# Squares turned by VectorE instead of TensorE transposes, and x loaded without its zeros, in a graph kernel on one core

## The chip, the cores and the metric

The kernel runs on one core of one Trainium2 chip. The metric is the device time in microseconds (us) of one execution. The core's engines are TensorE (PE; PEld is its loading of weights), VectorE (DVE), ScalarE (ACT), GpSimd (POOL) and SyncE (SP), which here issues most of the DMAs.

## What is computed

For each of B = 2048 samples, x is a 50 by 32 matrix (N nodes, D features). T = 2 maskers make an adjacency each, whose rows are divided by their sum; one step of a gated recurrence runs over the graph; batch and layer normalisation and an attention pooling follow. Cut to what matters:

```python
adj = einsum('bn,tnm->btm', x.reshape(b, 1600), masker_param) + masker_bias
adj = relu(adj).reshape(b, t, n, n)
adj = adj / (adj.sum(axis=-1, keepdims=True) + 1e-06)
m = einsum('btnd,de->btne', h, weight)
m = einsum('btnm,btmd->btnd', adj, m)
gates = m @ w_ih.T + b_ih + h @ w_hh.T + b_hh
# r, z, ng: sigmoid, sigmoid, tanh(r * ng)
h = (1.0 - z) * ng + z * h
# then normalisation over the batch, over the sample, softmax pooling over n
```

## The kernel before, in words

The samples are 16 tiles of 128. The program has three stages, each a block in which the engines run their own instruction streams against semaphores; between the blocks all engines meet.

**Stage 1** (`stage1`) computes the adjacency. The 100 rows of the two maskers are cut in 10 groups of GN = 10 rows, 500 columns wide; the tiles are cut in 2 blocks of 8. A *window* is one tile with one group: 160 windows, numbered c. In a window TensorE issues 38 matmuls of 128x500 (`window`, L445; x and the weights are each split in a high and a low part, `x_hi`, `x_lo`, `w_hi`, `w_lo`). ScalarE applies relu from PSUM into `u` (L307), VectorE sums the rows, adds epsilon, takes the reciprocal and multiplies into `an` (`normalise`, L357 to L365). `an` has the samples on its partitions. The next stage needs the column node m there, so TensorE turns it: after the fourth of its seven units of matmuls, window c runs four transposes of window c-1 (`transposes`, L427; 125 columns each), ScalarE copies them from PSUM to `at` (`evacuate`, L313), and SP stores `at` to the DRAM tensor `adjT` (`store_tile`, L204). The last window's transposes follow the loop. `u`, `an`, `at` and their PSUM banks are double: c2 is c % 2.

Beside this, ScalarE and VectorE split the weights of the next group in window w = 7 of each group (`split_w_hi` L287 and L288, `split_w_lo` L294 and L298), and split x of a tile (`split_x_hi`, `split_x_lo`, L259 to L272): in the first group x of tile w+1 in window w, and in the last group of the first block x of the second block. x comes through the one buffer `x_raw`, in two halves; SP issues `load_x` (L192) of a half when VectorE is done with the half before.

**Stage 2** (`stage2`) runs 8 iterations of two tiles, 8 rounds each; a round takes 4 samples of each quarter of the tile (QB = 4, 16 samples). In a round TensorE first aggregates for the next round (`aggregate`, L766): for each of 4 times 2 samples one float32 matmul, which the trace shows as two pairs of a weight load and a matmul. Its weights are x of one sample, `xs` (100 partitions by 64 columns); its moving operand is the adjacency of that sample, `adj` (100 partitions by 100 columns). The 100 partitions are the 50 nodes m for two samples at once, so that the weights are block diagonal: the upper 50 rows have their 32 features in the left 32 columns and zeros in the right, the lower the other way. Then come the gates' matmuls (`gates`, L793 and L799), and from the second tile on four transposes of the finished tile's h (L810). ScalarE makes the sigmoids and the tanh, VectorE the update, GpSimd the low part of x (L746).

`load_adj` and `load_xs` fill two slots r = 0, 1 by SP. `adj` is [100, 100, 64], sample last, read from `adjT` in runs of 64 floats (256 bytes); `xs` is [100, 64, 64], sample first, its zeros loaded from DRAM with the rest. Slot 0 is first filled in the last group of stage 1, slot 1 at the start of stage 2. TensorE waits for a slot (`adj_loaded`) at s == ROUNDS - 2 and s == S - 2 of an iteration, just after it has issued the aggregation of the slot's predecessor for round 7.

```python
if s == ROUNDS - 2:
    pe.wait_ge(adj_loaded[1], (it + 1) * 48)
if s == S - 2 and more:
    pe.wait_ge(adj_loaded[0], (it + 2) * 48)
pe.wait_ge(m_ready, it * S + s + 1)
```

**Stage 3** normalises and pools; the change does not touch it.

Of the kernel before, what the change touches and what calls it, by code (L numbers as in the profile page):

```python
# [25 lines left out]
P = 128  # L26
# [16 lines left out]
MPAD = 64  # L43
RK = 125
AK = GW // RK
assert AK * RK == GW and AK * P == 512
# [6 lines left out]
T_AT = 3  # L53
# [28 lines left out]
def wait(eng, sem, value):  # L82

    if not (isinstance(value, int) and value <= 0):
# [4 lines left out]
                              "fold_out par aw ab rowpar t_mask weights_loaded wd_ready bias_ready adj_loaded xg_loaded at_stored "  # L89
# [38 lines left out]
def load_adj(sp, shared, adjT, tile, r=0):  # L128

    for half in range(2):  # L130
        sp.dma_start(shared.adj[r][N * half:N * half + N], adjT[tile, :, SH * half:SH * half + SH].rearrange("(c m) s -> m c s", m=N)
                     ).then_inc(shared.adj_loaded[r], 16)


def load_xs(sp, shared, ins, tile, r=0):

    sp.dma_start(shared.xs[r][:], ins["xz"][tile]).then_inc(shared.adj_loaded[r], 16)
# [7 lines left out]
def stage1(nc, place, psum, ins, adjT, shared):  # L145
    xT, W, ident_d = ins["xT"], ins["W"], ins["ident"]
    with ExitStack() as ctx:  # L147
# [9 lines left out]
        ident = sb("ident_sb", [P, P])  # L157
        u = sb("u", [P, 2, GN, N])
        an = sb("an", [P, 2, GN, N])
        rows = sb("rows", [P, 3, GN])  # L160
        at = sb("at", [RK, 2, AK, P])
        assert free.at <= AT_WEIGHTS

        x_loaded, ident_loaded = [sem("x_loaded0"), sem("x_loaded1")], sem("ident_loaded")
# [4 lines left out]
        tr_done, at_ready = sem("tr_done"), sem("at_ready")  # L169
# [8 lines left out]

        def tr_out(c2):

            return psum[0:RK, (2 + c2) * BANK:(3 + c2) * BANK]
# [4 lines left out]
        def _(sp):  # L186
# [14 lines left out]
            def store_tile(c, c2, tile, group):  # L201

                sp.wait_ge(at_ready, c + 1)
                sp.dma_start(adjT[tile, bass.ds(group * GW, GW), :].rearrange("(k p) b -> p k b", p=RK),  # L204
                             at[:, c2]).then_inc(at_stored[c2], 16)
# [6 lines left out]
            sp.dma_start(ident[:, :], ident_d).then_inc(ident_loaded, 16)  # L212
            for dst, src in ((shared.wT4, "wT4"), (shared.wih, "wihT"), (shared.whh4, "whhT4"), (shared.biases, "biases")):
                sp.dma_start(dst[:], ins[src]).then_inc(shared.weights_loaded, 16)
            for blk in range(BLOCKS):
                for it, group in p1_iters(sp, blk):
                    for w in range(BLK):
# [20 lines left out]
                        if isinstance(it, int) and it == ITERS - 1:  # L238
# [5 lines left out]
                            if w == XS_TILES:  # L244
                                sp.wait_ge(mm_done, it * BLK + XS_TILES)
# [56 lines left out]
        def _(act):  # L302
# [6 lines left out]
            def evacuate(c, c2, start=False):  # L309
                act.wait_ge(tr_done, c + 1)  # L310
                if not start:
                    act.wait_ge(at_stored[c2], 8 * (c - c2))
                nc.scalar.copy(at[:, c2].rearrange("p k b -> p (k b)"), tr_out(c2)).then_inc(at_ready, 1)  # L313

# [5 lines left out]
            for blk in range(BLOCKS):  # L320
                for it, group in p1_iters(act, blk):
                    static = isinstance(it, int)
                    for w in range(BLK):
# [26 lines left out]
            evacuate(c, 1)  # L350

        @block.vector
        def _(dve):
            def normalise(c, c2, start=False):
# [31 lines left out]

            split_x_lo(dve, 0, 0)
# [1105 lines left out]
```

## Time and profile before

| | us |
|---|---|
| median of 3 runs | 2220.93 |
| range of the runs | 2220.83 to 2222.51 |
| the profiled execution: its own time | 2223.07 |
| the profiled execution: span from first to last instruction | 2221.3 |
| stage 1, from the trace | 0 to about 1459 |
| stage 2 | about 1460 to 2022 |
| stage 3 | the rest |

The profile gives for each engine the time in which it was busy. A matmul's recorded duration is longer than the distance to the next one, since matmuls are pipelined; what a matmul costs is read from the distance between starts. The granted clock is a share of 2.4 GHz: 1.00 is 2.4, 0.50 is 1.2 GHz. Line numbers (L445) are those of the kernel before unless the text says otherwise.

### The profile page before, as it was taken

Reading aid. Unit: us, or ns where it says so; the run is one execution under the profiler, and the core shown is the slowest. Engines: PE = TensorE matmul, PEld = TensorE weight load, DVE = VectorE, ACT = ScalarE, POOL = GpSimd, SP = SyncE. Lnnn points to the kernel's source line nnn. Section 1 sums busy time; section 2 is a strip of 40 time slices with the busy share of each in tenths; the row PEclk is TensorE's granted clock in tenths of the full one; section 3 lists DMA queues with packets and bytes.
Section 4 is the critical chain, followed back from the end, with each engine's and each line's share of the span. In section 5 each row is a group of like instructions: output and inputs, shape, how many; then the busy total and the mean of one; then the engine's idle time right before and its main releaser. Section 6 shows DMA issues by size and latency. Waiting matters only on the chain. (4 is left out here: it accounts for less than half of the span.)

```text
span 2221.3 us, 34738 instructions
## 1 busy us (share of the span) xinstructions
PE 2167.1 (98%) x12334; PEld 1721.3 (77%) x12334; DVE 1088.7 (49%) x2209; ACT 956.7 (43%) x1631; POOL 67.3 (3%) x68
## 2 busy tenths in 40 slices
PE   8999999999999999999999999989999999996898
PEld 7888888888888888888888888867777777775333
DVE  4432233323333433233322333238888888888667
ACT  4321222212223322122221222158888888895862
POOL 0000000000000000000000000010101111010000
PEclk9999999999999999999999999989999999998999
DMA  6412222122205321222212221457776676774660
GB/s 220 157 43 77 92 92 82 41 93 92 92 28 193 125 95 37 85 92 92 74 48 95 92 91 29 118 125 185 189 204 177 193 194 184 197 205 152 191 183 8
DMA packets 341777, 264.48 MB, mean 119 GB/s; under 512 B 169340, under 2 KB 303004, under 8 KB 339996
## 3 DMA queue, kind: packets, MB, share of 16 engines
q1 hardware_dynamic: 323580, 226.12, 34.7%
q10 hardware_dynamic: 18144, 37.69, 5.2%
q8 instruction: 29, 0.48, 0.1%
q14 instruction: 24, 0.20, 0.0%
HBM read 196.08 MB, written 67.70 MB: 119 GB/s over the span
## 5 line engine op out<-in xcount | busy, mean ns | idle before, releaser
L445 PE MATMUL psum<-w_hi,x_lo 128*128 128x500 f32 x2080 | 821.0, 395 | 8.0 <-DVE w_lo L294 8.0
L445 PE MATMUL psum<-w_lo,x_hi 128*128 128x500 f32 (+1 forms) x2080 | 808.3, 389 | 0.0
L445 PE MATMUL psum<-w_hi,x_hi 128*128 128x500 f32 x1920 | 744.0, 388 | 0.0
L357 DVE TENSOR_REDUCE rows<-u 128x10 f32<-128x500 f32 x160 | 107.5, 672 | 887.0 <-ACT u L307 886.4
L445 PEld LDWEIGHTS psum<-w_hi,x_lo 128*128 128x128 f32 x2080 | 391.5, 188 | 82.3 <-issue 8.0
L445 PEld LDWEIGHTS psum<-w_lo,x_hi 128*128 128x128 f32 (+1 forms) x2080 | 391.9, 188 | 72.2
L445 PEld LDWEIGHTS psum<-w_hi,x_hi 128*128 128x128 f32 x1920 | 360.9, 188 | 73.0
L313 ACT COPY at<-psum 125x512 f32<-125x512 f32 x160 | 93.5, 584 | 676.6 <-PE psum L427 676.6
L307 ACT ACTIVATE u<-psum 128x500 f32<-128x500 f32 x160 | 93.8, 586 | 341.3 <-PE psum L445 341.3
L766 PE MATMUL psum<-adj_sb,xs_sb 100*64 100x100 f32 x2048 | 200.6, 350 | 1.6 <-PEq L147 1.6
L766 PEld LDWEIGHTS psum<-adj_sb,xs_sb 100*64 100x64 f32 x2048 | 144.4, 149 | 45.6 <-issue 35.3
L629 ACT ACTIVATE r_gate<-psum,bias 64x400 f32<-64x400 f32 x256 | 151.0, 590 | 22.9 <-PE psum L793 20.8
L288 ACT CAST w_hi<-w_raw 128x1000 fp32r<-128x1000 f32 (+1 forms) x140 | 136.1, 972 | 46.0 <-PE psum L445 44.5
L294 DVE TENSOR_TENSOR w_lo<-w_raw,w_hi 128x1000 fp32r<-128x1000 f32 x120 | 144.0, 1200 | 23.6 <-ACT w_hi L288 15.9
L634 ACT ACTIVATE psum<-psum,bias 64x400 f32<-64x400 f32 x256 | 142.3, 556 | 14.0 <-DVE hG L689 7.1
L746 POOL TENSOR_TENSOR xg_lo<-xg_sb,xg_hi 128x400 fp32r<-128x400 f32 x64 | 67.1, 1051 | 1926.3 <-ACT xg_hi L595 1926.3
L365 DVE TENSOR_TENSOR an<-u,rows 128x500 f32<-128x500 f32 x160 | 108.6, 679 | 6.9
L697 DVE BATCH_NORM_STATS2 stats<-hC 128x128 f32 (+1 forms) x400 | 88.4, 282 | 47.1 <-ACT hC L607 46.6
L427 PEld LDWEIGHTS psum<-ident_sb,an 128*125 128x125 f32 x640 | 94.9, 188 | 16.4 <-DVE an L365 3.0
L427 PE MATMUL psum<-ident_sb,an 128*125 128x128 f32 x640 | 96.5, 274 | 3.4 <-DVE an L365 3.4
L674 DVE SCALAR_TENSOR_TENSOR n_in<-psum,bias,r_gate 128x400 f32<-128x400 f32 x128 | 79.5, 621 | 14.1 <-PE psum L799 13.6
L1127 DVE SCALAR_TENSOR_TENSOR pr<-h,nmu_sb,psum 128x512 f32<-128x512 f32 x100 | 70.0, 742 | 27.9 <-PE psum L1308 26.7
(169 smaller groups left out, 2135.1 us busy)
## 6 DMA issues: line engine op xcount, KB each, us to landing
w_raw<-W SPq DMA_DIRECT2D x140, 500.0 KB, 7.9
adjT<-at SPq DMA_DIRECT2D x160, 250.0 KB
adj_sb<-adjT SPq DMA_DIRECT2D x32, 1250.0 KB
xs_sb<-xz SPq DMA_DIRECT2D x16, 1600.0 KB
hF<-hC ACTq DMA_DIRECT2D x96, 256.0 KB, 6.3
h<-hF SPq DMA_DIRECT2D x64, 256.0 KB, 4.2
xg_sb<-xg ACTq DMA_DIRECT2D x14, 800.0 KB, 8.0
h<-hF SPq DMA_DIRECT2D x48, 192.0 KB, 3.4
```

What stands on the lines that cost most here:

```text
L288: nc.scalar.copy(w_hi[:, k0:k1, :], w_raw[:, k0:k1, :]).then_inc(w_hi_ready, 1)
L294: nc.vector.tensor_tensor(w_lo[:, k0:k1, :], w_raw[:, k0:k1, :], w_hi[:, k0:k1, :].bitcast(fp32), ALU.subtract).then_inc(w_ready, 1)
L307: nc.scalar.activation(u[:, c2].rearrange("p n m -> p (n m)"), mm_out(c2), ACT.Relu).then_inc(u_ready, 1)
L313: nc.scalar.copy(at[:, c2].rearrange("p k b -> p (k b)"), tr_out(c2)).then_inc(at_ready, 1)
L357: nc.vector.tensor_reduce(rows[:, 0], u[:, c2], AX.X, ALU.add).then_inc(dve_step, 1)
L365: nc.vector.tensor_tensor(an[:, c2], u[:, c2], rows[:, 2].unsqueeze(2).to_broadcast([P, GN, N]), ALU.mult).then_inc(an_ready, 1)
L427: last = nc.tensor.transpose(tr_out(c2)[:, k * P:(k + 1) * P], flat[:, k * RK:(k + 1) * RK], ident[:, :])
L445: last = nc.tensor.matmul(mm_out(w % 2), a[0:r, w, k, :], b[0:r, k, :], start=k == 0 and n == 0, stop=k == KF and n == 1)
L629: last = nc.scalar.activation(r_gate[half], rz_bank(pair)[half], ACT.Sigmoid, bias=bias[half, R_G:R_G + 1])
L634: last = nc.scalar.activation(z_bank[half], rz_bank(pair)[other], ACT.Sigmoid, bias=bias[other, Z_G:Z_G + 1])
L697: last = nc.vector.bn_stats(stats[:, bass.ds(tile, 1), c, :].rearrange("p i v -> p (i v)"), hC[:, c, :])
L766: last = nc.tensor.matmul(out_[SH * i:SH * i + SH, :, gi], xs[r][:, b, :], adj[r][:, :, b], start=True, stop=True)
```

## The change

Stage 1: TensorE's four transposes per window, their PSUM banks, ScalarE's copy out of them and the identity matrix are gone. Instead VectorE turns `an` with one `nc.vector.transpose`, which turns each square of 32 partitions by 32 columns in itself (`turn_squares`). For this `an` is padded from 50 to 64 columns per row (cleared once), and is single. `at` then has on partition 32i + m' the node m = 32k + m' of the 32 samples of quarter i, as [128, 2 (k), 10, 32]. `adjT` takes that shape, and is written in runs of 320 floats and read in runs of 3200.

Stage 2: `adj` becomes [100, 2, 100, 32], with the same order (sample last, 32 of them). `xs` becomes [100, 2, 32, 64]: half, feature, sample. Only the two diagonal blocks are loaded, from `x2`, which has no zeros; the rest is cleared once per slot by GpSimd, slot 0 in stage 1's last group, slot 1 between the first two tiles' `x_lo`. In the aggregation the step between two elements of the moving operand falls from 64 to 32 floats, and the step between two columns of the weights rises from 1 to 64 floats.

```diff
...
-        sp.dma_start(shared.adj[r][N * half:N * half + N], adjT[tile, :, SH * half:SH * half + SH].rearrange("(c m) s -> m c s", m=N)
-                     ).then_inc(shared.adj_loaded[r], 16)
+        for k in range(MB):
+            m0, m1 = TB * k, min(TB * k + TB, N)
+            sp.dma_start(shared.adj[r][N * half + m0:N * half + m1].rearrange("p i c s -> p i (c s)"),
+                         adjT[tile, k, SH * half:SH * half + SH].rearrange("(i m) c s -> m i (c s)", m=TB)[0:m1 - m0]
+                         ).then_inc(shared.adj_loaded[r], 16)
 
 
 def load_xs(sp, shared, ins, tile, r=0):
 
-    sp.dma_start(shared.xs[r][:], ins["xz"][tile]).then_inc(shared.adj_loaded[r], 16)
+    for half in range(2):
+        sp.dma_start(shared.xs[r][N * half:N * half + N, half], ins["x2"][tile, half]).then_inc(shared.adj_loaded[r], 16)
...
-        an = sb("an", [P, 2, GN, N])
+        an = sb("an", [P, GN, MPAD])
-        at = sb("at", [RK, 2, AK, P])
+        at = sb("at", [P, 2, MB, GN, TB])
...
             def store_tile(c, c2, tile, group):
 
                 sp.wait_ge(at_ready, c + 1)
-                sp.dma_start(adjT[tile, bass.ds(group * GW, GW), :].rearrange("(k p) b -> p k b", p=RK),
-                             at[:, c2]).then_inc(at_stored[c2], 16)
+                sp.dma_start(adjT[tile, :, :, bass.ds(group * GN, GN), :].rearrange("k p n s -> p k (n s)"),
+                             at[:, c2].rearrange("p k n s -> p k (n s)")).then_inc(at_stored[c2], 16)
...
-            sp.dma_start(ident[:, :], ident_d).then_inc(ident_loaded, 16)
...
-                                sp.wait_ge(mm_done, it * BLK + XS_TILES)
+                                sp.wait_ge(shared.xs_cleared[0], 1)
                                 load_xs(sp, shared, ins, 0)
...
-            def evacuate(c, c2, start=False):
-                act.wait_ge(tr_done, c + 1)
-                if not start:
-                    act.wait_ge(at_stored[c2], 8 * (c - c2))
-                nc.scalar.copy(at[:, c2].rearrange("p k b -> p (k b)"), tr_out(c2)).then_inc(at_ready, 1)
...
-                            for i in range(0, T_AT + 1):
-                                split_w_hi(act, i, it + 1)
-                        if not (static and it == 0 and w == 0):
-                            evacuate(c - 1, (w - 1) % 2, start=static and it == 0 and w <= 2)
-                        if split:
-                            for i in range(T_AT + 1, NU):
+                            for i in range(NU):
                                 split_w_hi(act, i, it + 1)
...
-            evacuate(c, 1)
...
-                if not start:
-                    dve.wait_ge(tr_done, c - 1)
-                nc.vector.tensor_tensor(an[:, c2], u[:, c2], rows[:, 2].unsqueeze(2).to_broadcast([P, GN, N]),
+                if not first:
+                    dve.wait_ge(at_ready, c)
+                nc.vector.tensor_tensor(an[:, :, 0:N], u[:, c2], rows[:, 2].unsqueeze(2).to_broadcast([P, GN, N]),
                                         ALU.mult).then_inc(an_ready, 1)
+
+            def turn_squares(c, c2, start=False):
+
+                dve.wait_ge(an_ready, c + 1)
+                if start:
+                    dve.wait_ge(an_cleared, 1)
+                else:
+                    dve.wait_ge(at_stored[c2], 8 * (c - c2))
+                nc.vector.transpose(at[:, c2], an[:].rearrange("p n (k s) -> p k n s", s=TB)).then_inc(at_ready, 1)
...
+            nc.vector.memset(an[:, :, N:MPAD], 0.0).then_inc(an_cleared, 1)
...
-                            normalise(c - 1, (w - 1) % 2, start=static and it == 0 and w <= 2)
+                            normalise(c - 1, (w - 1) % 2, first=static and it == 0 and w == 1)
+                            turn_squares(c - 1, (w - 1) % 2, start=static and it == 0 and w <= 2)
...
+            turn_squares(ITERS * BLK - 1, 1)
+
+        @block.gpsimd
+        def _(pool):
+            pool.wait_ge(mm_done, (ITERS - 1) * BLK + XS_TILES)
+            nc.gpsimd.memset(shared.xs[0][:], 0.0).then_inc(shared.xs_cleared[0], 1)
...
-            def transposes(c, c2, start=False):
-                pe.wait_ge(an_ready, c + 1)
-                if not start:
-                    pe.wait_ge(at_ready, c - 1)
-                flat = an[:, c2].rearrange("p n m -> p (n m)")
-                for k in range(AK):
-                    last = nc.tensor.transpose(tr_out(c2)[:, k * P:(k + 1) * P], flat[:, k * RK:(k + 1) * RK], ident[:, :])
-                last.then_inc(tr_done, 1)
...
-                    if none_before and i == NU - 1:
-                        pe.wait_ge(ident_loaded, 16)
-                    if i == T_AT and not none_before:
-                        transposes(c - 1, (w - 1) % 2, start=start)
...
-            transposes(ITERS * BLK - 1, 1)
...
             load_xg(sp, shared, ins, 1, 1)
             load_adj(sp, shared, adjT, 1, 1)
+            sp.wait_ge(shared.xs_cleared[1], 1)
             load_xs(sp, shared, ins, 1, 1)
             for c2 in range(2):
...
             x_lo(0, 0)
+            nc.gpsimd.memset(shared.xs[1][:], 0.0).then_inc(shared.xs_cleared[1], 1)
             x_lo(1, 1)
...
                 for gi in range(QB):
                     for i in range(2):
                         b = 32 * i + q * QB + gi
-                        last = nc.tensor.matmul(out_[SH * i:SH * i + SH, :, gi], xs[r][:, b, :], adj[r][:, :, b], start=True, stop=True)
+                        last = nc.tensor.matmul(out_[SH * i:SH * i + SH, :, gi], xs[r][:, :, :, b].rearrange("p h d -> p (h d)"), adj[r][:, i, :, q * QB + gi], start=True, stop=True)
...
                 if s == ROUNDS - 2:
-                    pe.wait_ge(adj_loaded[1], (it + 1) * 48)
+                    pe.wait_ge(adj_loaded[1], (it + 1) * 96)
                 if s == S - 2 and more:
-                    pe.wait_ge(adj_loaded[0], (it + 2) * 48)
+                    pe.wait_ge(adj_loaded[0], (it + 2) * 96)
                 pe.wait_ge(m_ready, it * S + s + 1)
...
-    adjT = nc.dram_tensor("adjT", [TILES, TN * N, P], fp32, kind="Internal").ap()
+    adjT = nc.dram_tensor("adjT", [TILES, MB, P, TN, TB], fp32, kind="Internal").ap()
...
-            slots = [(place(f"adj_sb{r}", [2 * N, TN, SH], AT_H + r * A_SLOT),
-                      place(f"xs_sb{r}", [2 * N, SH, 2 * D], AT_H + r * A_SLOT + TN * SH)) for r in range(2)]
+            slots = [(place(f"adj_sb{r}", [2 * N, SH // TB, TN, TB], AT_H + r * A_SLOT),
+                      place(f"xs_sb{r}", [2 * N, 2, D, SH], AT_H + r * A_SLOT + TN * SH)) for r in range(2)]
...
-        a = x.reshape(TILES, 2, 2, 32, N, D).transpose(2, 0, 4, 1, 3, 5).reshape(2, TILES, N, SH, D)
-        z = np.zeros_like(a[0])
-        return np.stack([np.concatenate([a[0], z], axis=-1), np.concatenate([z, a[1]], axis=-1)], axis=1).reshape(TILES, 2 * N, SH, 2 * D)
+        return x.reshape(TILES, 2, 2, 32, N, D).transpose(0, 2, 4, 5, 1, 3).reshape(TILES, 2, N, D, SH)
...
```

VectorE's instructions in an early window of stage 1, the first group, in which x is split too. Before:

```order
L357 TENSOR_REDUCE rows<-u 128x10 [waits u_ready]
L359 TENSOR_SCALAR rows<-rows 128x10 [waits dve_step]
L361 RECIPROCAL rows<-rows 128x10 [waits dve_step]
L365 TENSOR_TENSOR an<-u,rows 128x500 [waits tr_done,dve_step]
L269 TENSOR_TENSOR x_lo<-x_raw,x_hi 128x1024 [waits x_hi_ready]
L269 TENSOR_TENSOR x_lo<-x_raw,x_hi 128x512 [waits x_hi_ready]
L272 TENSOR_TENSOR x_lo<-x_raw,x_lo 64x128
```

The changed kernel (its own line numbers):

```order
L341 TENSOR_REDUCE rows<-u 128x10 [waits u_ready]
L343 TENSOR_SCALAR rows<-rows 128x10 [waits dve_step]
L345 RECIPROCAL rows<-rows 128x10 [waits dve_step]
L349 TENSOR_TENSOR an<-u,rows 128x10x50 [waits at_ready,dve_step]
L359 STREAM_TRANSPOSE at<-an 128x640 [waits an_cleared,an_ready]
L265 TENSOR_TENSOR x_lo<-x_raw,x_hi 128x1024 [waits x_hi_ready]
L265 TENSOR_TENSOR x_lo<-x_raw,x_hi 128x512 [waits x_hi_ready]
L268 TENSOR_TENSOR x_lo<-x_raw,x_lo 64x128
```

One instruction of 640 elements per partition joins VectorE's stream after the multiplication, ahead of the splitting of x, and the wait for TensorE (`tr_done`) is gone.

SP's DMAs at the start of stage 2, up to the refill of slot 0 (`adj_sb_49` and `adj_sb_51` are slots 0 and 1 of the adjacency, `xs_sb_52` slot 1 of x). Before:

```order
L560 DMA ident_sb<-ident 128x128
L142 DMA xg_sb<-xg 128x1600
L131 DMA adj_sb_51<-adjT 50x100x64 x2
L137 DMA xs_sb_52<-xz 100x4096
L131 DMA adj_sb_49<-adjT 50x100x64 [waits ax_done,at_stored1,at_stored0]
```

The changed kernel:

```order
L546 DMA ident_sb<-ident 128x128
L144 DMA xg_sb<-xg 128x1600
L131 DMA adj_sb_51<-adjT 32x2x3200
L131 DMA adj_sb_51<-adjT 18x2x3200
...
L139 DMA xs_sb_52<-x 50x2048 [waits xs_cleared1]
L139 DMA xs_sb_52<-x 50x2048
L131 DMA adj_sb_49<-adjT 32x2x3200 [waits ax_done,at_stored1,at_stored0]
```

(The two loads of the adjacency stand there twice, once per half; one pair is shown.) The loads of `xs` halve in size and now stand behind GpSimd's clearing.

## Rows read from the trace of the kernel before

**Rows 1.** Stretches: PE, PEld, DVE, ACT, POOL busy; clock, DMA share, GB/s

```profile
13.00:1458.00 1445.00, 1441.62 (x6710) 1209.76 (x6710) 463.31 (x848) 351.42 (x535) 0.00 (x0) 1.00 0.27 89
1458.00:1998.00 540.00, 533.26 (x4482) 422.88 (x4482) 450.77 (x1008) 467.33 (x889) 67.08 (x64) 0.98 0.72 189
```

**Rows 2.** Timeline, stage 1: TensorE around one window's transposes (start, length)

```profile
403.18 0.39 PE L445 MATMUL psum<-w_hi,x_hi 128*128 128x500 f32 x1
403.40 0.60 PE L427 MATMUL psum<-ident_sb,an 128*125 128x128 f32 x4
403.76 0.48 PE L445 MATMUL psum<-w_hi,x_lo 128*128 128x500 f32 x1
404.07 0.39 PE L445 MATMUL psum<-w_lo,x_hi 128*128 128x500 f32 x1
```

**Rows 3.** Timeline, stage 1: ScalarE's relu, the first and last of four

```profile
109.67 0.59 ACT L307 ACTIVATE u<-psum 128x500 f32<-128x500 f32 x1 [2.58 <-PE psum L445]
...
136.72 0.59 ACT L307 ACTIVATE u<-psum 128x500 f32<-128x500 f32 x1 [2.52 <-PE psum L445]
```

**Rows 4.** Groups of instructions: busy, mean ns, idle before and releaser

```profile
L357 DVE TENSOR_REDUCE rows<-u 128x10 f32<-128x500 f32 x160 | 107.5, 672 | 887.0 <-ACT u L307 886.4
...
L708 DVE STREAM_TRANSPOSE hT<-hG 128x800 f32<-128x800 f32 x64 | 64.0, 1004 | 1.7
```

**Rows 5.** Timeline, first group: one turn of x's only buffer

```profile
26.78 1.28 SPq L192 DMA_DIRECT2D x_raw<-xT  x2
34.12 1.83 DVE L269 TENSOR_TENSOR x_lo<-x_raw,x_hi 128x1024 fp32r<-128x1024 f32 x2 [3.13 <-ACT x_hi L259]
35.87 1.12 SPq L192 DMA_DIRECT2D x_raw<-xT  x2
37.54 0.59 ACT L307 ACTIVATE u<-psum 128x500 f32<-128x500 f32 x1 [2.05 <-PE psum L445]
```

**Rows 6.** Timeline from the end of stage 1 into stage 2

```profile
1456.71 0.68 DVE L365 TENSOR_TENSOR an<-u,rows 128x500 f32<-128x500 f32 x1
1457.45 1.11 PE L427 MATMUL psum<-ident_sb,an 128*125 128x128 f32 x4 [2.56 <-DVE an L365]
1458.59 0.58 ACT L313 COPY at<-psum 125x512 f32<-125x512 f32 x1 [3.08 <-PE psum L427]
1460.15 2.97 PE L766 MATMUL psum<-adj_sb,xs_sb 100*64 100x100 f32 x32 [1.59 <-PEq L147]
1461.95 4.04 POOL L746 TENSOR_TENSOR xg_lo<-xg_sb,xg_hi 128x400 fp32r<-128x400 f32 x4 [1461.50 <-ACT xg_hi L595]
```

**Rows 7.** Timeline, first tile of stage 2: SP's loads, TensorE in rounds 5 to 7

```profile
1460.84 13.45 SPq L131 DMA_DIRECT2D adj_sb<-adjT  x2
1474.33 7.24 SPq L137 DMA_DIRECT2D xs_sb<-xz  x1
1484.73 1.57 PE L766 MATMUL psum<-adj_sb,xs_sb 100*64 100x100 f32 x16
1488.79 1.57 PE L766 MATMUL psum<-adj_sb,xs_sb 100*64 100x100 f32 x16
1494.16 0.70 PE L793 MATMUL psum<-m_hi,wd_lo 64*128 64x400 f32 x2 [3.80 <-issue]
1498.70 1.57 PE L766 MATMUL psum<-adj_sb,xs_sb 100*64 100x100 f32 x16
```

**Rows 8.** Timeline, a later round of stage 2: TensorE's weight loads and matmuls

```profile
1603.73 1.21 PEld L766 LDWEIGHTS psum<-adj_sb,xs_sb 100*64 100x64 f32 x16 [0.27 <-issue]
1603.73 1.57 PE L766 MATMUL psum<-adj_sb,xs_sb 100*64 100x100 f32 x16
```

**Rows 9.** One microsecond in each aggregation (columns as in rows 1)

```profile
1461.00:1462.00 1.00, 1.00 (x16) 1.00 (x14) 0.00 (x0) 0.99 (x4) 0.05 (x1) 0.50 0.54 127
1604.00:1605.00 1.00, 1.00 (x16) 0.85 (x12) 0.76 (x2) 0.96 (x3) 0.00 (x0) 1.00 0.80 179
```

**Rows 10.** Groups: the aggregation's weight loads

```profile
L766 PEld LDWEIGHTS psum<-adj_sb,xs_sb 100*64 100x64 f32 x2048 | 144.4, 149 | 45.6 <-issue 35.3
```

More of the change, by code:

```diff
@@ L42 @@
 ITERS = BLOCKS * GROUPS
[L43 to L46, printed above, removed]
+TB = 32
+MB = -(-N // TB)
+MPAD = MB * TB
 SH = P // 2
@@ L52 @@
 NU = len(UNITS)
-T_AT = 3
 XH = 8
@@ L88 @@
 Shared = namedtuple("Shared", "adj xs xg wd wd_hi wd_lo wT4 wih whh4 biases bias h stats ident quarter score_mask square_mask "
-                              "fold_out par aw ab rowpar t_mask weights_loaded wd_ready bias_ready adj_loaded xg_loaded at_stored "
+                              "fold_out par aw ab rowpar t_mask weights_loaded wd_ready bias_ready adj_loaded xg_loaded at_stored xs_cleared "
                               "early_loaded h_loaded")
@@ L145, in stage1 @@
 def stage1(nc, place, psum, ins, adjT, shared):
-    xT, W, ident_d = ins["xT"], ins["W"], ins["ident"]
+    xT, W = ins["xT"], ins["W"]
     with ExitStack() as ctx:
@@ L156, in stage1 @@
         w_lo = sb("w_lo", [P, KC, GW], fp32r)
-        ident = sb("ident_sb", [P, P])
         u = sb("u", [P, 2, GN, N])
-        an = sb("an", [P, 2, GN, N])
+        an = sb("an", [P, GN, MPAD])
         rows = sb("rows", [P, 3, GN])
-        at = sb("at", [RK, 2, AK, P])
+        at = sb("at", [P, 2, MB, GN, TB])
         assert free.at <= AT_WEIGHTS
-        x_loaded, ident_loaded = [sem("x_loaded0"), sem("x_loaded1")], sem("ident_loaded")
+        x_loaded = [sem("x_loaded0"), sem("x_loaded1")]
         w_loaded = [sem(f"w_loaded{i}") for i in range(NU)]
@@ L168, in stage1 @@
         mm_done, u_ready, an_ready = sem("mm_done"), sem("u_ready"), sem("an_ready")
-        tr_done, at_ready = sem("tr_done"), sem("at_ready")
+        an_cleared, at_ready = sem("an_cleared"), sem("at_ready")
         at_stored = shared.at_stored
@@ L177, in mm_out @@
             return psum[:, c2 * BANK:c2 * BANK + GW]
-        def tr_out(c2):
-            return psum[0:RK, (2 + c2) * BANK:(3 + c2) * BANK]
         block = ctx.enter_context(nc.Block())
@@ L349, in _, with normalise @@
             relu(c, 1)
-            evacuate(c, 1)
         @block.vector
         def _(dve):
-            def normalise(c, c2, start=False):
+            def normalise(c, c2, first=False):
                 dve.wait_ge(u_ready, c + 1)
@@ L417, in _, with window @@
             normalise(ITERS * BLK - 1, 1)
+            turn_squares(ITERS * BLK - 1, 1)
[3 more added lines that the diff above has]
+            nc.gpsimd.memset(shared.xs[0][:], 0.0).then_inc(shared.xs_cleared[0], 1)
         @block.tensor
         def _(pe):
-            def transposes(c, c2, start=False):
-                pe.wait_ge(an_ready, c + 1)
-                if not start:
-                    pe.wait_ge(at_ready, c - 1)
-                flat = an[:, c2].rearrange("p n m -> p (n m)")
-                for k in range(AK):
-                    last = nc.tensor.transpose(tr_out(c2)[:, k * P:(k + 1) * P], flat[:, k * RK:(k + 1) * RK], ident[:, :])
-                last.then_inc(tr_done, 1)
-            def window(it, w, blk, c, start=False, bank_free=False, none_before=False):
+            def window(it, w, blk, c, bank_free=False):
                 pe.wait_ge(x_ready, 2 * (blk * BLK + w) + 1)
@@ L463, in _ @@
                         c = it * BLK + w
-                        window(it, w, blk, c, start=static and it == 0 and w <= 2,
-                               bank_free=static and it == 0 and w < 2, none_before=static and it == 0 and w == 0)
-            transposes(ITERS * BLK - 1, 1)
+                        window(it, w, blk, c, bank_free=static and it == 0 and w < 2)
 def p1_iters(eng, blk):
@@ L818, in turn @@
                     gates(it, s, more)
-            pe.wait_ge(adj_loaded[0], 48)
+            pe.wait_ge(adj_loaded[0], 96)
             aggregate(0)
@@ L1411, in program @@
                 adj_loaded=[sem("adj_loaded0"), sem("adj_loaded1")], xg_loaded=[sem("xg_loaded0"), sem("xg_loaded1")],
-                at_stored=[sem("at_stored0"), sem("at_stored1")], early_loaded=sem("early_loaded"),
+                at_stored=[sem("at_stored0"), sem("at_stored1")], xs_cleared=[sem("xs_cleared0"), sem("xs_cleared1")], early_loaded=sem("early_loaded"),
                 h_loaded=[[sem(f"h_loaded{p}{i}") for i in range(QC)] for p in range(2)])
@@ L1469 @@
         "ident": np.eye(P, dtype=x.dtype),
-        "xz": pairs(x),
+        "x2": pairs(x),
         "xg": x.reshape(TILES, 4, ROUNDS, QB, N, D).transpose(0, 1, 5, 2, 4, 3).reshape(TILES, P, ROUNDS, N * QB),
```

## The prediction

> **What bounds the kernel now.** I read first the stretches by stage. In stage 1 TensorE is busy 1441.6 of 1445 us at full clock, while VectorE is busy 463 and ScalarE 351, and the DMA engines at 0.27; in stage 2 TensorE is busy 533 of 540, ScalarE 467, VectorE 451, and the DMA share is 0.72 [rows 1]. So TensorE sets the pace of both, and what leaves its stream in stage 1 should come off the end. Then the timelines: around a window's transposes [rows 2], for the length of a window [rows 3], at the seam of the stages [rows 6], at the one place in stage 2 where TensorE stands still [rows 7], and in an aggregation [rows 8, 9], whose weights the change strides.
>
> **The transposes leave TensorE.** From the start of the matmul ahead of them (403.18) to the start of the second behind them (404.07) are 0.89 us [rows 2]. Two 128x500 matmuls lie in it besides the four transposes. The matmul ahead keeps 0.22 to its successor; 38 matmuls at 0.225 would be 8.57 us, and a window measures (136.72 - 109.67) / 3 = 9.017 us [rows 3]. Both give 0.44 us per window: 0.89 - 0.45, and 9.017 - 8.57. 159 of the 160 sets lie inside the loop: 159 x 0.44 = **-70.0 us**. Bounds: 0.36 us by the distance of starts alone (57 us), 0.48 if the slower matmul behind counts in full (76). I take 0.44, since window and gap agree.
>
> **The squares on VectorE.** The nearest row is the same instruction on 800 elements, 1.004 us [rows 4]; for 640 that is about 0.80 us, 160 x 0.80 = 129 us. VectorE waited 887 us for ScalarE's relu ahead of its row sums [rows 4], so it costs nothing there. It is also late for nobody. Even in window 7, where seven weight splits follow, VectorE gets 0.85 us later to work that TensorE wants only when window 7 is over, and the loop has a whole window (8.6 us) of slack. ScalarE drops its 0.58 us copy per window, which gains nothing, as ScalarE waits for TensorE. If this cover were gone, 0.80 us per window would stand in the place of 0.44.
>
> **First group.** Here x passes through one buffer: load issued at 26.78, splitting over at 35.95, next load at 35.87, so a turn takes 9.09 us, and the next window starts shortly before the relu at 37.54, about 1.2 us after the splitting ends [rows 5]. With windows of 8.57 us this turn is the slower one. SP now waits less (the store's wait ends on VectorE 6 us earlier), but the load, the cast and the subtraction stay. Seven windows at up to 0.5 us too slow, less that lead: at worst +2.3, at best 0; I take **+1.0 us**.
>
> **The seam.** Behind the last multiplication (ends 1457.39) come transposes of 1.11 and a copy of 0.58, which ends at 1459.17 [rows 6]. A transpose on VectorE of 0.80 and 0.07 of semaphore ends at 1458.26: **-0.9 us** (0 to -1.2).
>
> **The standstill at 1490.** Aggregations of the first tile follow each other at 1484.73 and 1488.79, 4.06 us, but the next is at 1498.70, 9.91 us later [rows 7]: 5.85 us lost, 3.8 of them idle and the rest by matmuls at half clock after it. TensorE waits there for slot 1, whose adjacency takes SP 13.45 us to issue in runs of 256 bytes and whose x follows at 1474.33 [rows 7]. Now the adjacency comes in runs of 12.8 kB and x is half as much. x waits for GpSimd's clearing of 4096 elements, which stands behind four x_lo that end at 1465.99 [rows 6]. GpSimd needs 1.01 us for 400 elements there, with two inputs; 4096 at that rate are 10.3 us, an upper end, so x can be issued at 1466 + 10.3 = 1476 at the latest, and the 7.24 us of the old, double load would still bring it in by 1484, ahead of 1490. So **-5.8 us**; at worst 0, if it is late by as much. The Trainium skill (DMA: Bandwidth & Descriptors, Specifications) asks for at least 512 bytes a transfer at line rate; the share of 0.72 in stage 2 fits that, and it is the shorter load, not the share, that gives time. Later tiles have their slots long before: no such wait shows, so DMA relief is worth 0 there.
>
> **The aggregation, 2048 pairs of weight load and matmul.** Weight columns now stand 256 bytes apart. The trace has no strided weight load, so bounds. At full clock 16 matmuls of 0.35 us span 1.57, a pair every (1.57 - 0.35) / 15 = 0.081 us; at half clock [rows 9] 32 span 2.97, every (2.97 - 0.35) / 31 = 0.085 us [rows 6, 8]. Halving TensorE's clock hardly changed the pace, so at full clock something other than the array bounds it, and weight loads have room beneath it. A load of 64 columns is recorded at 149 ns [rows 10] with its pipelining, and at least follows at 81. If striding adds nothing that isn't hidden: 0, the lower end. The upper: the whole recorded 149 in place of 81 ns, 2048 x 68 ns = +139 us. I take **0**, since the moving operand already strides by 256 bytes at 0.81 ns a column, and 64 weight columns at that pace are 52 ns, under 81. The moving operand's smaller step is taken as 0 too.
>
> Against this speaks the Trainium skill (SBUF — State Buffer, Door 1: The DMA port swizzle): SBUF is read in 16-byte lines, and each access that crosses to a new line pays a penalty, so that four floats is as far as a stride is free. By that rule every weight column now pays. The same page (Who interferes with whom) gives TensorE separate read ports for weights and moving operand, by which the load stays hidden as I take it. No row decides between the two.
>
> **Sum**, against the profiled execution's own 2223.07: -70.0 + 1.0 - 0.9 - 5.8 = -75.7, or 2147.4. That execution stands 2.1 above the median 2220.93, so the forecast is **2145 us**. A change under 0.2% (4.4 us) can't be told from none.
>
> **Rivals.**
> (a) *Weight loads partly show.* If a strided load needs 105 ns (64 columns at 1.64 ns, the moving operand's pace if the two samples of a pair run side by side), a pair goes from 81 to 105: 2048 x 24 = +49 us, about 2194. For: the rule above, and the aggregation's pace that doesn't follow the clock. Against: nothing shows that weights are read at that pace.
> (b) *Weight loads and moving operand share one way* and add up: 64 columns at 0.81 ns, 52 ns on each of 2048 pairs, +107 us, **2252, slower**. It ends on the other side from 81 + 75.7 / 2.048 = 118 ns a pair. Stage 2 would be 107 us longer, and ScalarE and VectorE idle in it. For: the pace fits a shared limit as well. Against: at half clock the array alone would explain 85 ns, so nothing has to be added.
> (c) *The smaller step of the moving operand speeds the aggregation.* TensorE would give way to ScalarE, busy 467 of 540: a gain of at most some 30 us, 2115.
> (d) *The standstill stays*, since clearing or the three waits in SP's stream delay slot 1: 2151.
> (e) *The transposes were hidden* and don't come off: rows 2 and 3 speak against it, since window length is the sum with them; under 0.01.
>
> **Chances.** Forecast 0.64 (own range 2138 to 2154, by the 0.36 to 0.48 and the small terms), (d) 0.05, (a) 0.14, (b) 0.10, (c) 0.07. The range must leave out 2 in 10: forecast, (d) and most of (a) are 0.80, so it reaches from 2132 to 2200. Faster 0.87 (all but (b) and the top of (a)), same 0.03, slower 0.10.
>
> **What will show it.** Windows of 8.57 us between relus in stage 1, no TensorE idle before a VectorE releaser; VectorE 129 us busier there; a transpose row near 0.80 us; first group windows up to 9.1; no gap near 1415 to 1425, where the first tile's rounds 6 and 7 will lie; aggregations still 16 in 1.57 us, and 4.06 apart in the first tile. Wrong would be: relus 9 us apart, or aggregations of over 1.6 us, which decide for (a) at about 1.9 and for (b) at 2.3; shorter ones mean (c).

## The result, and the profile after

The changed kernel takes 2247.56 us (2246.21 to 2249.74, four runs) against 2221.72 (2220.83 to 2223.71, four runs): ratio 1.0116, 95% interval 1.0098 to 1.0134. It is **slower by 26 us**, where 2145 with a range of 2132 to 2200 was forecast. The profiled execution took 2248.84, with a span of 2247.1.

Stretches by stage, columns as in [rows 1] (the seam of the stages now lies at 1386):

```profile
13.00:1386.00 1373.00, 1369.74 (x6071) 1138.96 (x6069) 593.08 (x1009) 260.92 (x377) 3.52 (x1) 1.00 0.29 101
1386.00:2050.00 664.00, 633.00 (x4708) 526.17 (x4708) 482.22 (x1064) 491.10 (x931) 70.20 (x65) 0.97 0.53 141
```

Stage 1 gave what was hoped for, and stage 2 took more than that back. Stage 1's relus on ScalarE, to be read beside [rows 3] (the first of four and the fourth):

```profile
104.76 0.59 ACT L303 ACTIVATE u<-psum 128x500 f32<-128x500 f32 x1 [7.99 <-PE psum L437]
...
130.48 0.59 ACT L303 ACTIVATE u<-psum 128x500 f32<-128x500 f32 x1 [7.99 <-PE psum L437]
```

(130.48 - 104.76) / 3 = 8.573 us a window. Groups of instructions; the first row is new, the others are to be read beside [rows 4] and [rows 10]:

```profile
L359 DVE STREAM_TRANSPOSE at<-an 128x640 f32<-128x640 f32 x160 | 135.3, 846 | 13.3
L341 DVE TENSOR_REDUCE rows<-u 128x10 f32<-128x500 f32 x160 | 107.7, 673 | 738.9 <-ACT u L303 738.8
...
L754 PEld LDWEIGHTS psum<-adj_sb,xs_sb 100*64 100x64 f32 x2048 | 220.8, 222 | 39.8 <-issue 38.5
```

VectorE turns the squares of a window in 0.846 us and still waits 739 us in all for ScalarE, so they cost nothing. The weight loads of the aggregation went from 149 to 222 ns. The seam and the first tile, to be read beside [rows 6] and [rows 7]:

```profile
1385.28 0.84 DVE L359 STREAM_TRANSPOSE at<-an 128x640 f32<-128x640 f32 x1
1387.12 4.09 PE L754 MATMUL psum<-adj_sb,xs_sb 100*64 100x100 f32 x32 [4.38 <-PEq L149]
1392.98 3.58 POOL L736 MEMSET xs_sb<- 100x4096 f32 x1
1396.59 0.67 SPq L139 DMA_DIRECT2D xs_sb<-x  x2
1416.99 2.09 PE L754 MATMUL psum<-adj_sb,xs_sb 100*64 100x100 f32 x16
1421.61 2.05 PE L754 MATMUL psum<-adj_sb,xs_sb 100*64 100x100 f32 x16
1426.18 2.05 PE L754 MATMUL psum<-adj_sb,xs_sb 100*64 100x100 f32 x16
```

The first aggregation starts at 1387.12, where it was at 1460.15 [rows 6]: 73.0 us gained. In the first tile aggregations follow each other every 4.6 us with no gap: the old standstill is gone. But 16 matmuls now take 2.05 to 2.17 us and not 1.57 [rows 8]. And TensorE stands still at places where it never did before. The first is at the top of the second iteration of stage 2's loop (timeline of VectorE and TensorE):

```profile
1548.23 1.73 PEld L754 LDWEIGHTS psum<-adj_sb,xs_sb 100*64 100x64 f32 x16 [0.27 <-issue]
1548.23 2.12 PE L754 MATMUL psum<-adj_sb,xs_sb 100*64 100x100 f32 x16
1555.71 0.57 DVE L651 TENSOR_TENSOR m_lo<-psum,m_hi 128x400 fp32r<-128x400 f32 x1 [7.30 <-issue]
1556.34 0.70 PE L781 MATMUL psum<-m_hi,wd_lo 64*128 64x400 f32 x2 [5.99 <-DVE m_lo L651]
...
1561.69 2.17 PE L754 MATMUL psum<-adj_sb,xs_sb 100*64 100x100 f32 x16
```

VectorE idles for 7.30 us with "issue" as the cause: the profile shows nothing that it waits for. TensorE waits 5.99 for VectorE's m_lo, and then runs at half clock (the last three columns are the granted clock, the DMA share and GB/s):

```profile
1548.00:1556.00 8.00, 2.35 (x18) 1.71 (x16) 0.70 (x2) 1.24 (x3) 0.00 (x0) 0.74 0.60 171
1556.00:1562.00 6.00, 5.66 (x25) 4.72 (x27) 4.12 (x8) 3.77 (x7) 0.00 (x0) 0.50 0.48 162
```

One aggregation to the next is 13.46 us here. Four more stand at 1635, 1721, 1807 and 1894 (12.72, 12.46, 13.39, 13.28), once in each iteration of stage 2's loop but the first. Among the waits (us in total, times, longest) and in the DMA queue that brings instructions (packets, MB, share) they show as:

```profile
DVE m_lo L651 <- issue: 35.8, 5, 7.3
...
q14 instruction: 49, 0.40, 0.1%
```

Before, that queue had 24 packets and 0.20 MB, and no such wait of VectorE stood in the list. The times of the packets say more. From 1610 to 1980 us, in the loop, that queue moved nothing in the kernel before; in the changed kernel the stretch from 1635 to 1980, which is four iterations, has

```profile
q14 instruction: 20, 0.16, 0.1%
```

which is five packets of 8 kB in each iteration, the first at the moment when VectorE stops (1548.1 at the standstill shown).

**The account.** From the first aggregation to the last start of one: before 2020.63 - 1460.15 = 560.5 us, after 2044.56 - 1387.12 = 657.4, so +97.0. The five standstills are 65.3 - 5 x 5.0 = 40.3 of it, where 5.0 is an undisturbed round of the changed kernel, and the vanished one is -5.9. What is left, 62.6, is 0.49 on each of 127 rounds, nearly what 16 matmuls grew (2.09 - 1.57 = 0.52). -73.0 + 97.0 = +24.0 of the 25.8 between the spans.

There are two theories for the two parts. **W**: TensorE reads weights with a large step more slowly, and that read does not hide beneath the read of the moving tile. **L**: the VectorE instructions added in stage 1 pushed stage 2's loop to a place in VectorE's program from which each iteration has to fetch code again. The Trainium skill (Runtime: NRT & Kernel Launch, Instruction fetch mechanics) has the rule for L: an engine holds two blocks of 256 instructions, and a branch to a place outside them waits for a fetch. The rival of L is that a DMA or one of the changed semaphores is late for VectorE; the rival of W is the adjacency, which lies otherwise too.

### The profile page after: what moved, and what is told of

Read it like the earlier page. It is cut to its first block and busy times, and to the rows that moved or that the text cites. A ratio compares the mean times of both kernels' runs of the same rounds, so it can differ in the third digit from the quotient of the medians.

```text
span 2247.1 us, 33291 instructions
## 1 busy us (share of the span) xinstructions
PE 2168.2 (96%) x11694; PEld 1732.1 (77%) x11694; DVE 1225.2 (55%) x2370; ACT 867.0 (39%) x1471; POOL 73.9 (3%) x70
## 5 line engine op out<-in xcount | busy, mean ns | idle before, releaser
L437 PE MATMUL psum<-w_hi,x_lo 128*128 128x500 f32 x2080 | 806.5, 388 | 7.9 <-DVE w_lo L290 7.9
L754 PE MATMUL psum<-adj_sb,xs_sb 100*64 100x100 f32 x2048 | 267.4, 423 | 4.4 <-PEq L149 4.4
L754 PEld LDWEIGHTS psum<-adj_sb,xs_sb 100*64 100x64 f32 x2048 | 220.8, 222 | 39.8 <-issue 38.5
L359 DVE STREAM_TRANSPOSE at<-an 128x640 f32<-128x640 f32 x160 | 135.3, 846 | 13.3
L290 DVE TENSOR_TENSOR w_lo<-w_raw,w_hi 128x1000 fp32r<-128x1000 f32 x120 | 137.7, 1191 | 4.1 <-ACT w_hi L284 3.4
L651 DVE TENSOR_TENSOR m_lo<-psum,m_hi 128x400 fp32r<-128x400 f32 x128 | 70.9, 554 | 40.9 <-issue 35.8
L781 PE MATMUL psum<-m_hi,wd_lo 64*128 64x400 f32 x256 | 58.8, 456 | 30.2 <-DVE m_lo L651 29.5
```

What stands on the lines that cost most here:

```text
L290: nc.vector.tensor_tensor(w_lo[:, k0:k1, :], w_raw[:, k0:k1, :], w_hi[:, k0:k1, :].bitcast(fp32), ALU.subtract).then_inc(w_ready, 1)
L359: nc.vector.transpose(at[:, c2], an[:].rearrange("p n (k s) -> p k n s", s=TB)).then_inc(at_ready, 1)
L437: last = nc.tensor.matmul(mm_out(w % 2), a[0:r, w, k, :], b[0:r, k, :], start=k == 0 and n == 0, stop=k == KF and n == 1)
L754: last = nc.tensor.matmul(out_[SH * i:SH * i + SH, :, gi], xs[r][:, :, :, b].rearrange("p h d -> p (h d)"), adj[r][:, i, :, q * QB + gi], ...
```

## The experiments

In the edits below, lines that the argument does not need are left out, and from before_strided on lines are cut to the part that changes.

**fill64: the code's place alone.** 64 instructions that do nothing of use (each clears one column) are added to VectorE's program, in stage 1's last group.

```diff
+                        if static and it == ITERS - 1:
+                            for n in range(8):
+                                nc.vector.memset(spare[:, w * 8 + n:w * 8 + n + 1], 0.0)
```

> The changed kernel with 64 one-column memsets (8 in each of the eight windows) added to VectorE's stream in stage 1's last group, where VectorE idles 4 us a window. Theory L (code loading): the changed VectorE stream puts the 289 instructions of its stage 2 loop 98 further on than before, so that the code of the loop is fetched again in each of its iterations, and VectorE stands 7.3 us at the top of five of them. Moved by 64 more, the loop fits again: the five standstills (13.4 us instead of 5.0 between two aggregations) go, 5 x 8.4 = -42 us, about 2206, and the page's instruction packets fall from 49 towards 24. Rival D (data): VectorE waits there for something of the data path, a load or TensorE; then 64 memsets in stage 1 change nothing, 2247 to 2250. Theory W (weights) says nothing here: aggregations stay at 2.1 us.

2208.81 us (2207.92 to 2209.98), ratio to before 0.9937 (0.992 to 0.9953). Adding work took 38.8 us off the changed kernel. VectorE's "issue" waits are gone, and the queue is back at

```profile
q14 instruction: 25, 0.20, 0.0%
```

From the first aggregation to the last start of one are 617.2 us in the place of 657.4, so 40.2 less, the 40.3 of the account. The aggregation stayed at 2.09. L holds, and W's part is separate.

**before_fill96: the same on the kernel before,** with 12 memsets a window, so that its loop starts where the changed kernel's does, within two instructions.

> The kernel before, nothing changed but 96 one-column memsets in VectorE's stream of stage 1's last group (12 a window, VectorE idles 5 us there), which puts its stage 2 loop where the changed kernel has it, within 2 instructions. Theory L (code loading): standstills of VectorE of 7 us at the top of the loop's iterations appear, +40 us, about 2262, and the instruction packets rise from 24 to about 49. Rival: the standstills need the new loads or the slower aggregation too; then 2222.

2261.69 us (2260.85 to 2263.03), ratio 1.0178 (1.0161 to 1.0195), so +39. The wait, and the queue:

```profile
DVE m_lo L667 <- issue: 33.1, 5, 6.6
...
q14 instruction: 50, 0.41, 0.1%
```

The standstills need neither squares nor strided weights. Counted in the programs as built, VectorE's loop is 289 instructions long and starts at instruction 596 before, 694 after, 692 here and 758 in fill64; only 692 and 694 are bad. The later kernels fit: xs_whole has its loop at 694 and the waits, the others have it at 596 or 758 and none. An estimate by the Trainium skill's blocks of 256: a loop of 289 lies in two blocks, or in three when it starts in the last 32 places of one, and an offset of 44 to 73 instructions ahead of the count puts just the two bad starts there. So the runs are consistent with that rule, but neither the offset nor the size of a block was measured; what they show is that the loop's place decides.

**before_strided: weights strided alone.** The kernel before, with x still loaded whole with its zeros, but laid out as [sample inside]; adjacency and squares untouched.

```diff
-place(f"xs_sb{r}", [2 * N, SH, 2 * D]
+place(f"xs_sb{r}", [2 * N, 2, D, SH]
-xs[r][:, b, :]
+xs[r][:, :, :, b].rearrange("p h d -> p (h d)")
```

> The kernel before with one thing alone: xs laid out as half, feature, sample (its zeros still loaded from DRAM), so that the weights' columns stand 64 floats apart; the moving operand keeps its step of 64, and VectorE's stream is untouched. W: aggregations of 2.1 us instead of 1.57, +66 us, about 2288, no standstills at the loop's top. M: 1.57 and 2221. If the moving operand's step has a part, it lies between.

2257.57 us (2254.63 to 2259.3), ratio 1.0153 (1.0136 to 1.017). 16 matmuls take 1.88 us, +0.31, and rounds about 4.37 us in the first tile and 4.78 later, in the place of 4.06 and 4.47. W holds, but at 0.31 and not at the expected 0.52: something else adds 0.21.

**xs_whole: weights adjacent alone.** The changed kernel with x loaded whole, zeros and all, sample by sample as before, and so without GpSimd's clearing.

```diff
-    for half in range(2):
-        sp.dma_start(shared.xs[r][N * half:N * half + N, half], ins["x2"][tile, half])
+    sp.dma_start(shared.xs[r][:], ins["xz"][tile])
-xs[r][:, :, :, b].rearrange("p h d -> p (h d)")
+xs[r][:, b, :]
```

> The changed kernel, but x of the second stage as before: loaded with its zeros, sample first, weights' columns next to each other, no clearing. Theory W (strided weights make the aggregation slow): 16 matmuls fall from 2.1 to 1.57 us, 127 x 0.52 = -66 us, about 2182; the five standstills of VectorE stay, since its stream is unchanged. Rival M (the moving operand's new step of 32 floats is what slows it): it stays at 2.1 us and the time at 2247. Rival S (both loads share one way, so striding adds to the moving operand): also 1.57, so W and S are not told apart here.

2255.25 us (2249.93 to 2256.55), ratio 1.014 (1.0123 to 1.0157). The aggregation takes 1.73: it lost 0.36 of its 0.52, and 0.16 stays, with weights as before. What differs from before in the aggregation is the moving tile, whose columns stand 32 floats apart and not 64. The time did not fall to the expected 2182, since a new wait came beside the five code waits, ScalarE's for xg (the x of the gates):

```profile
ACT xg_hi L575 <- DMA xg_sb<-xg: 37.5, 9, 6.4
```

**xs_whole_fill64: both undone,** the last kernel with the 64 memsets.

> Both edits at once: x as before and the 64 memsets. Theories L and W together: 2247.6 - 42 - 66 = 2140 us, which is the forecast of the prediction (2145) within 5 us. If L is wrong 2182; if W is wrong 2206; if neither holds 2247.

2234.63 us (2233.61 to 2234.81), ratio 1.0052 (1.0035 to 1.0069). The expectation missed by 95 us, more than any other. The code waits are gone and the aggregation is at 1.73, but ScalarE waits longer for xg, and TensorE for ScalarE:

```profile
ACT xg_hi L579 <- DMA xg_sb<-xg: 59.1, 13, 6.2
...
PE psum L777 <- ACT psum L618: 42.0, 13, 4.8
```

fill64, which differs in x and its weights alone, has no such wait and is 26 us faster in spite of its slower aggregation. So x without its zeros has a use that the prediction valued at nothing.

**xs_late: is it the burst?** SP issues a tile's adjacency in 1.4 to 2.0 us now, where it took 13.45 [rows 7] and later 9.4 to 9.8. So the whole x follows at once, and may take the DMA engines' time from xg. Here x's load waits three more rounds.

```diff
                         load_adj(sp, shared, adjT, tile + 2, r)
+                        sp.wait_ge(ax_done, (tile + 1) * ROUNDS + 3)
                         load_xs(sp, shared, ins, tile + 2, r)
```

> The changed kernel with x of the second stage whole (weights contiguous), the 64 memsets, and SP's load of x's slot held back by three rounds behind that of the adjacency. Theory Q (a burst in the queues): in xs_whole_fill64 ScalarE waits 59 us in 13 places for xg, whose load is issued on the other queue just as 2.5 MB of adjacency and 1.6 MB of x, now issued within 3 us instead of 17, fill the DMA engines. With x later xg lands in time: the 13 standstills of about 5 us go, 2234.6 - 60 = about 2172. Rival: xg is late for the adjacency's long runs alone; then 2230.

2211.61 us (2208.79 to 2215.25), ratio 0.9954 (0.9938 to 0.9971): 23 us better, some 40 short of what was expected. ScalarE still waits

```profile
ACT xg_hi L580 <- DMA xg_sb<-xg: 48.5, 14, 6.5
```

So the moment of x's load has a part in it; the rest of that wait stays open.

**steps_moving and steps_weights: the disputed cost by itself.** In both, each of the 16 rounds of an iteration reads its operands with steps of its own, so that the aggregation computes something else. All the rest, and the loads too, is as in fill64.

```diff
+                w_step, m_step, m_off, dense = PATTERNS[s]
...
-xs[r][:, :, :, b].rearrange("p h d -> p (h d)"), adj[r][:, i, :, q * QB + gi]
+flat_x[:, w0:w0 + 63 * w_step + 1:w_step], flat_a[:, m0:m0 + 99 * m_step + 1:m_step]
```

> A measurement inside the changed kernel with 64 memsets: the 16 rounds of an iteration aggregate with 16 different address patterns (so the aggregation computes something else). Weights contiguous throughout; the moving operand steps by 1, 2, 4, 8, 16, 32 floats with the two samples 3200 apart, then 32, 64, 33, 36, 40, 48 with them 32 apart, 3 (3200), 1 and 64 with the output dense instead of 4 floats apart, and 56. If the reading of the moving operand bounds the aggregation, 16 matmuls fall below 1.57 us at step 1 and the odd steps, and 32 is slower than 64 as in the run with x whole (1.73 against 1.57). If the write to PSUM with its 4-float step bounds it, all stay at 1.57 and only the two dense ones fall. If the instruction rate bounds it, all stay at 1.57. If step 32 at 3200 and at 32 apart differ, it is the distance of the two samples and not the step that costs.

> The same with the moving operand at step 64 as before, and the weights' columns 2, 4, 8, 16, 32, 33, 36, 64 and 63 floats apart, then pairs of steps weights/moving: 64/1, 64/32, 64/33, 36/36, 4/1, 64/4, and last 1/64 as before. A rule of 16-byte lines gives 1.57 up to step 4 and one higher value from 8 on (1.88 at 64, by the run before_strided). If banks matter, 33 and 63 are cheaper than 32 and 64. If the two reads share one way, 64/1 is no slower than 1/64; if each has its own, the weights' cost stays at about 0.3 us whatever the moving operand does.

Timeline rows of steps_moving, weights adjacent, moving steps of 1, 3, 4 and 64 floats:

```profile
1654.85 0.91 PE L765 MATMUL psum<-adj_sb,xs_sb 100*64 100x100 f32 x16
...
1650.63 1.30 PE L765 MATMUL psum<-adj_sb,xs_sb 100*64 100x100 f32 x16
...
1605.68 1.65 PE L765 MATMUL psum<-adj_sb,xs_sb 100*64 100x100 f32 x16
...
1628.60 1.57 PE L765 MATMUL psum<-adj_sb,xs_sb 100*64 100x100 f32 x16
```

and of steps_weights, weight steps of 64 and 63 beside a moving step of 64, and 64 beside a moving step of 1:

```profile
1632.10 1.88 PE L765 MATMUL psum<-adj_sb,xs_sb 100*64 100x100 f32 x16
...
1636.88 1.64 PE L765 MATMUL psum<-adj_sb,xs_sb 100*64 100x100 f32 x16
...
1641.10 1.15 PE L765 MATMUL psum<-adj_sb,xs_sb 100*64 100x100 f32 x16
```

All of them, the time of 16 matmuls in us at full clock:

| weight step | moving step: us |
|---|---|
| 1 | 1: 0.91; 2: 0.95; 3: 1.30; 4: 1.65; 8: 1.66; 16: 1.65; 32: 1.70 (1.77 with halves 3200 apart); 33: 1.65; 36: 1.64; 40: 1.78; 48: 1.59; 56: 1.69; 64: 1.57 |
| 2, 4, 8, 16, 32, 33, 36, 63, 64 | 64: 1.60, 1.67, 1.73, 1.75, 1.96, 1.68, 1.66, 1.64, 1.88 |
| 64 | 1: 1.15; 4: 1.72; 32: 2.12; 33: 1.77; 64: 1.88 |
| 4; 36 | 1: 1.19; 36: 1.71 |

The pairs (1, 64), (64, 64) and (64, 32) give back what before (1.57), before_strided (1.88) and the changed kernel (2.09) measured, the last within 0.03. How the output lies does not matter: the rounds above write it four floats apart, and with the output adjacent it is 0.91 at step 1 and 1.57 at step 64 as well. So the largest cost was in the kernel before already: its moving tile costs 1.57 where an adjacent one costs 0.91. Two expectations did not come. An odd moving step is not cheap as such (33 takes 1.65), and the weights show no edge at four floats: they rise from 1.60 at a step of 2 to 1.96 at 32. One run of each program took 2151.31 and 2158.43 us.

One more row of steps_moving matters. Its first 32 matmuls, 16 with a moving step of 1 and 16 with 2, run at a granted clock of 0.50 (timeline, and one microsecond with the columns of [rows 1]):

```profile
1387.72 2.94 PE L765 MATMUL psum<-adj_sb,xs_sb 100*64 100x100 f32 x32 [4.38 <-PEq L149]
...
1388.00:1389.00 1.00, 1.00 (x16) 1.00 (x15) 0.00 (x0) 0.99 (x3) 0.00 (x0) 0.50 0.82 270
```

The kernel before took 2.97 for 32 at that clock with a step of 64 [rows 6]. So the step costs next to nothing at half clock, and at full clock it sets the pace.

**adj_turned: the version that follows.** x stays as the change has it. VectorE writes each square with the group's 10 entries inside, and the matmul reads ten runs of ten; the bytes of stores and loads stay adjacent. The 64 memsets are in, so fill64 (2208.81 us) is what it is to be compared with.

```diff
-        at = sb("at", [P, 2, MB, GN, TB])
+        at = sb("at", [P, 2, MB, TB, GN])
-                nc.vector.transpose(at[:, c2], an[:]
+                nc.vector.transpose(at[:, c2].rearrange("p k s n -> p k n s"), an[:]
-adj[r][:, i, :, q * QB + gi]
+adj[r][:, i].rearrange("p c s -> p (c s)").rearrange("p (g s n) -> p g s n", g=GROUPS, s=TB)[:, :, q * QB + gi, :]
```

> The changed kernel with 64 one-column memsets in VectorE's program (as in fill64: 2208.8 us, 16 aggregation matmuls in 2.09 us) and one more edit: VectorE's transposition writes each square of 32 entries by 32 samples with the sample outside and the 10 entries of the group inside, so that in stage 2 the moving operand of an aggregation matmul is 10 runs of 10 adjacent floats instead of 100 floats 32 apart. Stores and loads move the same contiguous bytes. Theory S (a step between the elements that TensorE reads is what costs time, of the moving tile and of the weights): the probes read 0.91 us at step 1 and 0.95 at step 2 with adjacent weights, 1.57 to 1.78 at steps of 4 and more, and 1.15 with weights 64 apart beside an adjacent moving tile; so 16 matmuls in 1.15 to 1.30 us. 127 rounds by 0.79 to 0.94 are 100 to 119 us if the whole of it shows and some 77 to 92 us at the 77% that showed in the probe of moving steps: 2090 to 2132 us, most likely 2110. The rival R (the chip needs one step of one size per operand, every new run of ten starts afresh at the cost of a step): 1.9 to 2.1 us and 2200 to 2210 us. VectorE's transposition may take longer than 0.85 us for its scattered writes; at under 2 us it stays hidden in stage 1, whose first aggregation then still begins near 1388 us.

**2143.25 us** (2142.19 to 2144.22), ratio to before 0.9646 (0.9633 to 0.9659): 79 us faster than before and 66 faster than fill64. One round of it, the group of its turns on VectorE, and two waits:

```profile
1575.00 1.16 PE L758 MATMUL psum<-adj_sb,xs_sb 100*64 100x100 f32 x16
1576.50 0.45 PE L785 MATMUL psum<-m_hi,wd_lo 64*128 64x400 f32 x2 [0.34 <-DVE m_lo L655]
```

```profile
L360 DVE STREAM_TRANSPOSE at<-an 128x640 f32<-128x640 f32 x23 | 31.6, 1375 | 2.2
```

```profile
PE psum L785 <- ACT psum L625: 22.2, 56, 1.3
PE psum L785 <- DVE m_lo L655: 15.9, 47, 0.4
```

S, the theory that the step costs, is right and its rival R wrong: ten short runs, at 1.16 us, are as good as the one long run in steps_weights (1.15). The turn went from 0.846 to 1.375 us and stays hidden: the first aggregation starts at 1387.47, as in fill64 (1387.85). The time came out 11 us above the range. Of 127 x 0.93 = 118 us, 66 show (550.9 from first to last aggregation, 617.2 in fill64). 38 of the missing 52 are the two waits shown, for ScalarE's sigmoids and for VectorE's m_lo. TensorE was busy all the time from 1450 to 1990 us in fill64, and is busy for 443 of 480 us from 1450 here: TensorE alone no longer sets the round of 4.4 us.

## Why the prediction was wrong, point by point

- **Transposes, -70.0:** right. Windows of 8.573 us, 8.57 expected; with the seam the first aggregation came 73.0 us earlier, where -70.0 + 1.0 - 0.9 = -69.9 stood. The first group's +1.0 did not come: its windows are 8.57 us too.
- **Squares at no cost:** right. A turn takes 0.846 us for the 0.80 estimated, and VectorE still idles for 739 us.
- **The seam, -0.9:** right. `an` ends at 1385.24 and the turn at 1386.12, 0.88 later, where transposes and copy took 1.78.
- **The standstill at 1490, -5.8:** right. Clearing took 3.58 us, a third of its upper end.
- **The aggregation, "I take 0":** here it failed. The sum took 0 from bounds of 0 to +139, and it measures +0.52 us on 16 matmuls and 62.6 us over the 127 rounds. Two of its reasons fell. The first was that the weight read lies hidden beneath the matmul, at 52 against 81 ns: with weights 64 apart it shows with 0.31 us on 16 pairs, 19 ns a pair. The second was to read "Halving TensorE's clock hardly changed the pace" as room for the weights. The likeness of the two paces, 0.085 and 0.081 us, was chance: at half clock an adjacent tile is as slow (2.94 us for 32), and at full clock the moving tile's own step was the limit. A stride in the weights adds to it (1.57 to 1.88), as it does beside an adjacent tile (0.91 to 1.15). "The moving operand's smaller step is taken as 0 too" failed by 0.13 to 0.20 us at adjacent weights (1.70 to 1.77 against 1.57). The rule of the Trainium skill cited against the change (SBUF — State Buffer, Door 1: The DMA port swizzle) was the better guide, in part. Moving steps of 1, 2, 3 and 4 floats read 0.91, 0.95, 1.30 and 1.65, and from 4 to 64 the time stays between 1.57 and 1.78, as lines of 16 bytes with at least two hits each would have it. But that a stride of four floats is still free, as that section says, does not hold here: at four the price is paid in full. And the separate ports of the same page of the Trainium skill (Who interferes with whom) did not keep the two reads from adding.
- **The rivals:** (b) had the sign and nearly the time, 2252, by luck. It wanted 107 us of weights and aggregations of 2.3 us; the 103 us above the forecast are about 39 of code, 35 to 39 of weights, and the rest mostly the moving step, with aggregations of 2.09. (a) asked for 1.9 us an aggregation, which is what the weights alone do (1.88). (c) had the sign of the moving step wrong. Of (d), the standstill, and (e), hidden transposes, nothing came.
- **What no case held:** VectorE's code, +40 us. The prediction asked of each added VectorE instruction how long it runs, and never where the loop behind it would lie. None of the groups of rows could tell it; the length of the loop and the queue of instruction packets would have been the places to ask. Without it the kernel would have been at 2208.8, above the range still, and 14 us faster than before.

## What to carry to other kernels

For small float32 matmuls on strided views, cost both operands by their steps, and measure an adjacent version before calling the pace TensorE's. Here two floats apart was nearly free, and four apart cost as much as 64. The layout can often be had from an instruction that permutes anyway, as the transposition's output here. When a change adds or removes instructions ahead of a long hardware loop (289 instructions here), look for an "issue" wait at the top of each iteration and for instruction packets inside the loop. 64 idle instructions took 39 us off one kernel, and 96 put 39 us on another.

## What the runs showed of the hardware that was not expected

- Weight steps of 32 and 64 floats are dearer than their neighbours: 32 takes 1.96 us and 33 takes 1.68, 64 takes 1.88 and 63 takes 1.64. Beside weights 64 apart, a moving step of 32 takes 2.12 and one of 33 takes 1.77 (its halves lie otherwise as well). One float more or less is worth 0.24 to 0.35 us on 16 matmuls. Why was not tested.
- A wait for code stops VectorE for up to 7.6 us (xs_whole), and TensorE, idle 5.99 us after it in the changed kernel, goes on at a granted clock of 0.50, so that each such wait cost 8 us of time.
- At a granted clock of 0.50, 32 matmuls of the aggregation take 2.94 us with moving steps of 1 and 2 and 2.97 with 64; at full clock 16 take 0.91 with a step of 1 and 1.57 with 64.
- VectorE's transposition of 640 floats per partition takes 0.846 us into adjacent places and 1.375 into places ten floats apart.
